# Residual sum of the second attention: from a vector-engine add to a unit-matrix matmul with a scalar-engine copy

## The reference

```python
x = x + attn(layernorm(x), Wq, bq, Wk, bk, Wv, bv)          # 16 heads, 4 groups, causal
x = x + xattn(layernorm(x), ctx, ctx, Wc, bc)               # softmax(q k^T / 4) v, then @ Wc.T + bc
x = x + ffn(layernorm(x), gate_weight, Wg, Wu, Wd, Sg, Su, Sd)   # 6 of 64 experts, and shared ones
```

## Time and profile before

| | |
|---|---|
| median of 3 runs | 744.94 us (743.66 to 747.97) |
| span of the profiled execution | 738.7 us |
| PE / PEld / DVE / ACT busy over the span | 651.9 / 473.9 / 449.4 / 337.4 us |
| first and last of the 128 records of the projection (L476) | at 212.3 and 393.1 us |
| end of the attention block, start of the experts' block | about 418.8 us |

### The profile page before, as it was taken

The page is one execution under the profiler, slowest core; times in us unless marked ns, Lnnn a source line. Parts: engine busy times, 40 slices in busy tenths (PEclk is TensorE's granted clock), DMA queues, the critical chain, the costliest instruction groups (busy, mean ns, idle before and its releaser), DMA issues. The chain is left out here.

```text
span 738.7 us, 17020 instructions
## 1 busy us (share of the span) xinstructions
PE 651.9 (88%) x6417; PEld 473.9 (64%) x6417; DVE 449.4 (61%) x1142; ACT 337.4 (46%) x639; POOL 347.2 (47%) x380
## 2 busy tenths in 40 slices
PE   1699999999779988999989899889999999999790
PEld 0356666666567766666763366458888888788570
DVE  3166766757778788989974699503333334334247
ACT  2367777776657777767754433212222222222000
POOL 6012222212543344434312355487677777776473
PEclk9899999999999999999999999989999999999655
DMA  8231333355343332222311250028999999996598
GB/s 248 29 61 36 80 83 82 86 103 108 89 112 68 62 74 71 60 52 64 98 38 43 82 161 0 0 58 225 249 253 240 249 261 245 240 239 131 103 348 274
DMA packets 112064, 94.27 MB, mean 128 GB/s; under 512 B 59760, under 2 KB 95856, under 8 KB 111984
## 3 DMA queue, kind: packets, MB, share of 16 engines
q1 hardware_dynamic: 96368, 74.57, 37.4%
q0 software_dynamic: 10240, 14.16, 10.6%
q10 hardware_dynamic: 5376, 4.46, 1.9%
HBM read 60.26 MB, written 24.50 MB: 115 GB/s over the span
## 5 line engine op out<-in xcount | busy, mean ns | idle before, releaser
L1398 POOL DMA_INDIRECT sum_d<-outs,targets x64 | 91.8, 1434 | 36.8 <-issue 13.7
L786 DVE TENSOR_REDUCE mx<-Sc 128x16 f32<-128x1024 f32 x64 | 78.3, 1223 | 35.5 <-PE Sc L430 35.2
L1231 PE MATMUL Sc<-xT,wgu_sb 128*88 128x96 f32 x1024 | 95.0, 246 | 0.7 <-ACT xT L1317 0.7
L1231 PEld LDWEIGHTS Sc<-xT,wgu_sb 128*88 128x88 f32 x1024 | 89.3, 157 | 0.9 <-issue 0.8
L1468 DVE TENSOR_TENSOR hid<-sil,Sc 88x192 f32<-88x192 f32 x64 | 22.4, 350 | 110.5 <-ACT sil L1323 110.5
L654 ACT COPY ET<-ring 128x512 f32<-128x512 f32 x128 | 68.9, 589 | 40.5 <-PE ring L442 37.9
L458 PEld LDWEIGHTS O<-vbd,ET 128*64 128x64 f32 x2048 | 66.5, 138 | 29.5 <-issue 17.0
L790 DVE TENSOR_TENSOR E<-Sc,mx 128x1024 f32<-128x1024 f32 x64 | 78.4, 1225 | 6.9 <-DVE mx L786 0.5
L442 PE MATMUL ring<-ident,E 128*128 128x128 f32 x512 | 69.3, 279 | 12.3 <-ACT E L693 12.3
L458 PE MATMUL O<-vbd,ET 128*64 128x34 f32 x2048 | 73.6, 225 | 3.6 <-ACT ET L654 3.0
L430 PE MATMUL Sc<-kbd,qT 64*64 64x256 f32 x1024 | 71.6, 382 | 4.6 <-DMA kbd<-kT 4.6
(11 more groups left out here) (200 smaller groups left out, 1202.0 us busy)
## 6 DMA issues: line engine op xcount, KB each, us to landing
wgu_sb<-in_wgu_dram SPq DMA_DIRECT2D x64, 352.0 KB
wd_sb<-in_wd_dram SPq DMA_DIRECT2D x64, 176.0 KB
sum_d<-zeros SPq DMA_DIRECT2D x16, 524.0 KB, 5.5
kbd<-kT SPq DMA_DIRECT2D x248, 32.0 KB, 2.2
X<-in_x_dram SPq DMA_DIRECT2D x8, 512.0 KB, 6.5
rows_d<-xhT SPq DMA_DIRECT2D x8, 512.0 KB, 3.0
xnT<-sum_d SPq DMA_DIRECT2D x8, 512.0 KB, 8.8
out_dram<-X ACTq DMA_DIRECT2D x8, 512.0 KB, 3.7
```

The source lines that it names most:

```text
L786: nc.vector.reduce_max(mx[:, m % 2, :], sc, AX.X).then_inc(s_mx, 1)
L1231: last = nc.tensor.matmul(GP[e % 2][0:MH, CAP * u:CAP * (u + 1)], wgu[:, j, 4 * MH * c + MH * u:4 * MH * c + MH * (u + 1)], xT[:, e % 2, c ...
L1398: pool.indirect_dma_start(w["sums"][e % 2], bass.IndirectOffsetOnAxis(ap=targets[:, e:e + 1], axis=0), outs[:, e % EB, :], None, compute_o ...
```

## The change

The projection's bank takes three products in place of two: first x itself, as the product of the 128 x 128 unit matrix `ident` with the tile `X[:, m - NT, :]` (256 columns, float32), then the two halves of the projection, added onto it. The bank then holds the new x, and the scalar engine copies it over the tile, right after `probs`. The vector engine's sum is gone; its routing statistics now wait for the scalar engine's copy. The wait for the bias (`s_b`, every fourth tile) moves from the vector engine to TensorE, ahead of the unit matmul. In the ring the WC uses are counted among those that the scalar engine frees.

```diff
         if crossed(m - 2):
-            uses.append((("WC", m - 2), "dve"))
+            uses.append((("WC", m - 2), "act"))
...
             def wc(m):
                 out = empty_bank(("WC", m))
+                if m % GT == 0:
+                    pe.wait_ge(s_b, m // GT - NG + 1)
+                nc.tensor.matmul(out[:, 0:E], ident[:], X[:, m - NT, :], start=True, stop=False)
                 pe.wait_ge(*saved(("OT", m)))
                 for c in range(2):
                     last = nc.tensor.matmul(out[:, 0:E], oT[:, m % 2, c, :], w["wc_sb"][:, c, :],
-                                            start=c == 0, stop=c == 1)
+                                            start=False, stop=c == 1)
                 last.then_inc(s_fill, 1)
...
+            def wc(m):
+                name = ("WC", m)
+                act.wait_ge(s_fill, ring.filled(name))
+                nc.scalar.copy(X[:, m - NT, :], bank(name)[:, 0:E]).then_inc(s_act, 1)
+
             def probs(m):
...
                     probs(m)
+                if crossed(m - 2):
+                    wc(m - 2)
                 if m % 4 == 2 and routed((m - 10) // 4):
                     logit_exp((m - 10) // 4)
...
-            def wc(m):
-                name = ("WC", m)
-                dve.wait_ge(s_fill, ring.filled(name))
-                if m % GT == 0:
-                    dve.wait_ge(s_b, m // GT - NG + 1)
-                nc.vector.tensor_tensor(X[:, m - NT, :], bank(name)[:, 0:E], X[:, m - NT, :], ALU.add).then_inc(s_dve, 1)
-
             def route_stats(m):
                 n = m - NT
-                dve.wait_ge(s_dve, ring.saved(("WC", m))[1])
+                dve.wait_ge(*saved(("WC", m)))
                 nc.vector.bn_stats(rst[:, n % GT, :], X[:, n, :]).then_inc(s_rst, 1)
...
                     stats(gx, (m + 1) % 4)
-                if crossed(m - 2):
-                    wc(m - 2)
                 if is_self(gp):
```

## The result

The changed kernel took 754.71 us (median of four runs, 749.57 to 757.53) where before took 745.62; ratio 1.0122, interval 1.008 to 1.0164. Six further runs gave 752.71 and 1.0129 (1.0097 to 1.0161). It is slower by 1.2%: 9.1 between the medians, where 10.5 was forecast (755.4).

The account below looks back on a forecast made before the run. The prediction took TensorE (PE) in the attention block as the bound, stopped by waits for other engines. Its terms, 12.4 + 4.4 + 1.8 - 8.1 = +10.5 us, on 744.9 gave 755.4 us, range 748.5 to 762.

Parts of the forecast that it names:

- The bound: Attention block: its time is passed on whole; TensorE is the pace, idle 2.28 us a middle group in three waits.
- The unit matmul: Every step on TensorE: two more records, 0.43 us a step, paid in 29 of 32 steps, 12.4 us.
- The exponential: Step A's copy on ACT delays the exponential for B; PE's wait grows by 0.55 in eight groups, 4.4 us.
- The bank of WC: Steps B and D: TensorE's waits for the vector engine's sum to free this bank go, a credit of 8.1 us.
- The wait in C: Step C: transposes wait 0.4 us for later routing copies in groups 2 to 6, half in group 2; 1.8 us.
- The sum: Whole kernel: all terms together, 10.5 us slower; the middle group alone 0.7 us longer.
- The median of the runs lies 6.2 above the span, and I carry that over: Whole kernel: the 6.2 us between profiled span and median of the runs was assumed to stay after the change.
- DVE should be idle some 13 us more: Sign expected in the changed profile: 32 sums of 0.41 us gone from the vector engine, which ends no sooner.
- The open term: First group's DMA wait, shortened to 3.0 us: the clock might stay up, 1.7 us less; left out of the total.
- The vector engine was not the pace of before: Rival, attention block: vector engine is the pace, the added product hides and 8.1 us go, 736.8 us; chance 6%.
- The two halves did not cancel: Rival, attention block: added product paid, ACT has room, first group's clock stays up; +2.6 us, 747.5; chance 14%.
- The scalar engine did not become the pace: Rival, every step: ACT's wait for the projection and its copy reach PE, 11.6 us more, 767 us; chance 8%.

Follow-up runs that it names:

- exp_ahead_only: Changed kernel with the scalar engine's exponential for step B put ahead of the last two routing normalizings; median 750.3 us, ratio to before 1.0080.
- copy_later: Changed kernel with the scalar engine's copy to x moved behind the first normalizing (A, B, C) or the exponential (A, D); 748.9 us, ratio to before 1.0046.
- shared_sum: Against before: unit matmul and copy in B and D, vector engine's sum early in A and C, exponential for B ahead of two normalizings; 737.8 us, ratio 0.9907.

## Why the prediction was right

*The bound.* The block is passed on whole, and PE is the pace, stopped by three waits: shown by the unit matmul alone, which changed those waits to 0.25, 0.75 and none.

*The unit matmul.* 64 records, two of them 0.60, the projection 0.43 later: as taken from the row of its own form.

*The exponential.* 1.24 in place of 0.68, so 0.56 for a forecast 0.55, and the copy alone shows the same wait.

*The bank of WC.* Both waits gone, as credited. The credit and the unit matmul's full price belong together, as the forecast had them: alone the unit matmul is cheap because it uses up those same waits.

*The wait in C.* 0.18 by PE and about 0.4 by the weight loads (a row for which the profile names no releaser), in five groups; the forecast was 0.4 in groups 2 to 6.

*The sum.* For the middle group +0.7 was forecast, and 0.79 measured; the first was to take 24.8 and took 25.01 (23.90 in the second profile, where its wait for the DMA was 2.04 in place of 3.09). But before's own first group took 22.98 and 24.09, so in the second pair it did not grow at all: that it came out at 25.01 is in part luck. The mark moved by 13.2 and 9.4, 11.3 on average, for 10.5. In the first pair 1.7 of it is a fall of the clock in the last group that the first profile of before does not have (17.51 to 19.19 from A to the last projection, in its two profiles).

*What was off.* "The median of the runs lies 6.2 above the span, and I carry that over": 2.0 of it is what lies around the span, the other 4.2 most likely that the profiled execution was a quick one. It did no harm, because the forecast is before's median and a difference on top of it. The credit of 8.1 and the 0.4 in C are waits of the weight loads; PE's own were 6.3 (4.7 + 1.6) and 0.18 a group. In the middle group this evens out: 0.7 by the forecast's terms, 0.79 by PE's. "DVE should be idle some 13 us more": in the middle group it was idle for 3.99 in place of 2.47, but 0.79 of that is the group's own growth; the vector engine's busy time fell by 0.73 (22.28 to 21.55), not by 4 x 0.41 = 1.64. The rows of before (three) and after (two) behind the subtraction of step A show it:

```profile
308.58 0.42 DVE L775 BATCH_NORM_STATS2 ast<-X 128x6 f32<-128x256 f32 x1
308.92 0.41 DVE L815 TENSOR_TENSOR X<-ring,X 128x256 f32<-128x256 f32 x1
309.24 0.17 DVE L781 BATCH_NORM_AGGREGATE amv<-ast 128x2 f32<-128x6 f32 x1
```
```profile
314.25 0.42 DVE L785 BATCH_NORM_STATS2 ast<-X 128x6 f32<-128x256 f32 x1
314.70 0.18 DVE L791 BATCH_NORM_AGGREGATE amv<-ast 128x2 f32<-128x6 f32 x1
```

From the statistics to their aggregate it took 0.66 with the sum between, and takes 0.45 without: half of the sum lay where the aggregate waited for the statistics anyway.

*The open term.* With the unit matmul ahead of it, the DMA wait of the first group left PE idle for 3.09, and the clock did not stay up; nor did it in the second profile of the changed kernel, behind 2.04 (0.59 over 218 to 222). The 1.7 stay lost there, and the forecast without them was the right one:

```profile
218.20 1.09 PE L430 MATMUL Sc<-kbd,qT 64*64 64x256 f32 x16 [3.09 <-DMA kbd<-kT]
...
219.00:223.00 4.00, 4.00 (x23) 3.48 (x16) 2.96 (x4) 1.54 (x3) 0.85 (x1) 0.57 0.95 199
```

But exp_ahead_only, with the same unit matmul ahead of the same wait, kept the clock:

```profile
217.59 1.09 PE L430 MATMUL Sc<-kbd,qT 64*64 64x256 f32 x16 [3.04 <-DMA kbd<-kT]
...
218.00:222.00 4.00, 4.00 (x56) 3.18 (x46) 3.04 (x5) 2.19 (x5) 1.29 (x1) 1.00 1.19 250
```

And in copy_later it fell behind 1.58 (0.58 over 218 to 222). So the length of this idle time alone does not settle whether the clock falls. The prediction rightly left the term open; that the 1.7 stayed lost it had not worked out.

*The rivals.* The vector engine was not the pace of before, but it was near: as soon as PE's waits in B went, it stopped the kernel at 23.83. The Trainium skill (Perfetto Trace Analysis, "Identifying the Most-Contended Engine") would have had that engine relieved first, by its occupancy. Here the change that relieved it made the kernel slower. In the form where TensorE waits for nothing its weight loads fill 18.52 of 23.89 (78%), the vector engine 21.17 (89%), and yet TensorE is the pace: two unit matmuls less and two sums more on the vector engine made the group 0.6 shorter. The measurement decides: neither share says which of the two sets the pace, the waits do. The two halves did not cancel: each alone costs little or gains, together they cost 0.80 in a middle group. The scalar engine did not become the pace: its wait for the projection, 22.7 in 32 steps, reached PE through the exponential and the copies to xnT alone.

## What to carry to other kernels

Where two engines are nearly full, price a change by the waits between them and count each wait once: two changes that use up the same wait do not add up, and either alone can look harmless. Work given to an engine at its queue's wrong place costs more than its duration: the 0.37 copy made the exponential 0.98 late because it first waited for a full bank. And where moving work from one engine to another only moves the limit, share it: in the groups where both engines are full, half of it on each was 0.6 shorter than all on either; where the vector engine had room, all of it there was shorter.

## What the runs showed of the hardware

Behind one and the same wait of 1.71 TensorE's clock fell to 1.2 GHz in one execution and not in another, at a price of 1.7 us. Behind the DMA wait of the first group it fell after 1.58, 2.04, 3.09 and 3.39 of idle time and stayed up after 2.84 (shared_sum) and 3.04, in six profiles of five kernels. The Trainium skill (TensorE: Matmul & The Clock Gate, "Why this matters for your kernels") asks to avoid idle gaps between bursts of matmuls lest the clock fall; the trace agrees in part, since like gaps were followed by a fall in some executions and not in others. In the order of its instructions here the vector engine was at its limit with 22.14 of 23.83 busy: short gaps between its own instructions made up 1.5, and it waited 0.2 for TensorE.
